# A scan for the routing prefixes, a later weight copy on GpSimd, last tiles one by one, and products that nobody reads on TensorE

## The reference

```python
Y = einsum(where(causal, softmax(Q K^T / 4), 0), V)
x = layernorm(x + Y)
probs = softmax(x @ router^T);  topk_probs, selected = top_k(probs, 2)
topk_probs = topk_probs / max(topk_probs.sum(-1), EPS)
# sort the 8192 choices by expert; keep the 1280 heaviest of each expert
expert_inputs[e, slot] = x[token]
expert_out = ((expert_inputs @ w1^T) * silu(expert_inputs @ wg^T)) @ w2^T
out[token] += expert_out[e, slot] * kept_w
x = layernorm(x + out)
```

## Time and profile before

| | us |
|---|---|
| median of 3 runs | 1727.33 |
| lowest, highest | 1725.76, 1728.22 |
| the profiled execution, its own time | 1726.38 |
| its span in the trace | 1724.6 |
| TensorE busy in the span | 1623.0 (94%) |
| VectorE busy | 1139.5 (66%) |
| ScalarE busy | 1255.3 (73%) |
| GpSimd busy | 300.3 (17%) |

### The profile page before, as it was taken

The page is one execution under the profiler, slowest core; times in us unless marked ns, Lnnn a source line. Parts: engine busy times, 40 slices in busy tenths (PEclk is TensorE's granted clock), DMA queues, the critical chain, the costliest instruction groups (busy, mean ns, idle before and its releaser), DMA issues. The chain is left out here.

```text
span 1724.6 us, 31303 instructions
## 1 busy us (share of the span) xinstructions
PE 1623.0 (94%) x12878; PEld 952.0 (55%) x12878; DVE 1139.5 (66%) x1762; ACT 1255.3 (73%) x1350; POOL 300.3 (17%) x247
## 2 busy tenths in 40 slices
PE   8989999999999999999999994699999999999995
PEld 6823333333333333333333344589998988889884
DVE  7857777777777878777868679345445444644475
ACT  7879999999999999999999986233333333433333
POOL 1000000000000000000310000524243425425144
PEclk9989999999999999999999997899999999999998
DMA  7691030300300303003021003213143323323043
GB/s 252 220 265 56 11 79 1 83 7 1 88 1 3 87 1 78 11 1 88 2 99 50 1 12 111 98 38 107 15 113 68 67 58 68 104 46 92 4 134 121
DMA packets 78385, 118.28 MB, mean 69 GB/s; under 512 B 8690, under 2 KB 62299, under 8 KB 78222
## 3 DMA queue, kind: packets, MB, share of 16 engines
q1 hardware_dynamic: 63328, 98.32, 19.2%
q0 software_dynamic: 14880, 17.82, 5.8%
q10 hardware_dynamic: 32, 0.07, 0.0%
HBM read 80.22 MB, written 40.37 MB: 70 GB/s over the span
## 5 line engine op out<-in xcount | busy, mean ns | idle before, releaser
L975 DVE TENSOR_REDUCE sums<-expq 128x1 f32<-128x1536 f32 (+7 forms) x576 | 559.6, 1034 | 175.7 <-ACT expq L945 175.3
L945 ACT ACTIVATE probs<-scores 128x1536 f32<-128x1536 f32 (+1 forms) x384 | 509.2, 1478 | 8.5 <-PE scores L841 8.4
L945 ACT ACTIVATE expq<-scores 128x1536 f32<-128x1536 f32 x320 | 447.4, 1536 | 2.5 <-PE scores L841 0.9
L863 PE MATMUL o_ps<-probs,v 128*32 128x256 f32 (+1 forms) x4864 | 348.0, 368 | 0.0
L1597 ACT ACTIVATE gate<-up_ps 128x512 f32<-128x512 f32 x128 | 76.6, 598 | 324.8 <-PE up_ps L1434 317.7
L841 PE MATMUL scores<-aq,ak 98*128 98x512 bf16 (+3 forms) x1280 | 304.8, 353 | 7.8 <-PEq L621 6.4
L841 PE MATMUL scores<-ak,aq 98*128 98x512 bf16 (+3 forms) x1184 | 265.1, 343 | 22.7 <-ACT probs L945 16.9
L841 PEld LDWEIGHTS scores<-aq,ak 98*128 98x128 bf16 x1280 | 95.2, 98 | 212.4 <-ACT expq L945 75.5
L1434 PE MATMUL up_ps<-xeT_hi,wup_hi 128*128 128x512 f32 x512 | 203.3, 397 | 3.1 <-DVE xeT_lo L1818 1.4
L1914 DVE TENSOR_TENSOR mid<-up_ps,gate 128x512 f32<-128x512 f32 x128 | 88.4, 691 | 175.8 <-ACT gate L1597 162.0
L1434 PE MATMUL up_ps<-xeT_lo,wup_hi 128*128 128x512 f32 x512 | 202.3, 395 | 0.0
(11 more groups left out here) (269 smaller groups left out, 1903.8 us busy)
## 6 DMA issues: line engine op xcount, KB each, us to landing
raw<-w_T SPq DMA_DIRECT2D x16, 1024.0 KB
split_dram<-parts SPq DMA_DIRECT2D x16, 768.0 KB, 4.8
aq<-split_dram SPq DMA_DIRECT2D x42, 256.0 KB
ak<-split_dram SPq DMA_DIRECT2D x42, 256.0 KB
raw<-wg_T SPq DMA_DIRECT2D x8, 1024.0 KB
v_dram<-vst SPq DMA_DIRECT2D x8, 544.0 KB, 6.8
v<-v_dram SPq DMA_DIRECT2D x8, 544.0 KB, 9.7
xT<-x_T SPq DMA_DIRECT2D x8, 512.0 KB, 6.4
```

The lines of the kernel that those rows point to most:

```text
L863: last = nc.tensor.matmul(o_ps[g % O_RING][32 * h:32 * h + 32, col:col + w], value(gg, k, h, 32), probs[:, m % 2 * GH + h, at:at + w], sta ...
L945: nc.scalar.activation(dst, src[:, 0:w], ACT.Exp, scale=HD ** -0.5).then_inc(exp_done, 1)
L975: last = nc.vector.tensor_reduce(sums[:, gg % 2, col, h:h + 1], expq[:, at % X_RING, lo:lo + w], AX.X, ALU.add)
```

## The change

Five edits, all in the last block:

1. **The places.** `first_prefixes` takes the place of `prefixes` for the first pass. A tensor `by_tile` holds for each expert its base and then the 32 totals; `goes_on` is 1.0 everywhere and 0.0 at the start of each expert. One `tensor_tensor_scan` over 8 x 33 = 264 elements gives in `starts` the base plus the sum of the totals of the earlier tiles. GpSimd fills `goes_on` and the bases at the start of the block (three more instructions, and `iota_ready` is waited for at 11 instead of 8). The sum of all tiles (`total`) is now taken from `starts` in `count_over`.
2. **GpSimd's copy.** `split_down(0, 0)` moves from `keep_ready` to behind the first fetch.
3. **The last tiles** leave as (0, 1), then 2, then 3.
4. **Unread products.** TensorE runs `unread(n)`: n fp32 products of `ident` with the 512 columns of `after` (a constant mask), written to a bank of `up_ps` whose content nobody reads. 3 of them when `logit_off` is there, 14 behind the prefix products, 14 behind the eight list pieces, and 1 behind the first transposes.
5. The branch for an overfull expert, which these inputs don't take, adds the base itself.

```diff
+UNREAD = (3, 14, 14, 1)
...
-        LAST_TILES = ((0, 1), (2, 3))
+        LAST_TILES = ((0, 1), (2,), (3,))
...
+                pool.memset(goes_on[:], 1.0).then_inc(iota_ready, 1)
+                pool.wait_ge(iota_ready, 9)
+                pool.memset(goes_on[:, :, 0:1], 0.0).then_inc(iota_ready, 1)
+                nc.gpsimd.tensor_copy(by_tile[:, :, 0:1], ebase[:][:, :, None]).then_inc(iota_ready, 1)
...
-
-                pool.wait_ge(keep_ready, 1)
-                split_down(0, 0)
...
                 fetch(0, slot_row[:, 0:CT])
+                split_down(0, 0)
                 set_rows(0, 0, 1)
...
+                def unread(n):
+                    for _ in range(n):
+                        nc.tensor.matmul(up_ps[1][:, 1, :], ident[:], after[:].rearrange("p r k -> p (r k)"), start=True, stop=True)
+
+                pe.wait_ge(logit_off, 1)
+                unread(UNREAD[0])
                 pe.wait_ge(keep_ready, 1)
                 prefix_products(ALL).then_inc(prefix_ready, 1)
+                unread(UNREAD[1])
...
+                unread(UNREAD[2])
                 pe.wait_ge(xin_loaded[0], 16 * NA)
                 turn(0, 0)
+                unread(UNREAD[3])
...
+                def first_prefixes(link):
+
+                    dve.wait_ge(prefix_ready, 1)
+                    link(nc.vector.tensor_copy(by_tile[:, :, 1:TT + 1], pf_ps[:, 1, :, :].rearrange("p t e -> p e t")))
+                    link(nc.vector.tensor_tensor_scan(starts[:].rearrange("p e t -> p (e t)"), goes_on[:].rearrange("p e t -> p (e t)"),
+                                                      by_tile[:].rearrange("p e t -> p (e t)"), 0.0, ALU.mult, ALU.add))
+                    link(nc.vector.tensor_tensor(pos[:], starts[:, :, 0:TT].rearrange("p e t -> p t e"), pf_ps[:, 0, :, :], ALU.add))
...
-                    link(nc.vector.tensor_tensor(pos[:, tiles, :], pos[:, tiles, :], each(ebase, tiles), ALU.add))
...
-                    upto_tile = prefixes(link, 1, tiles)
-                    link(nc.vector.tensor_copy(total[:], upto_tile[:, TT - 1, :]))
+                    first_prefixes(link)
                     places(link, tiles)
...
+                    link(nc.vector.tensor_tensor(total[:][:, :, None], starts[:, :, TT:TT + 1], ebase[:][:, :, None], ALU.subtract))
```

More of the change, by code:

```diff
@@ L1130, in program @@
             pos = sb(st, "pos", [P, TT, E])
+            goes_on, by_tile, starts = (sb(st, s, [P, E, TT + 1]) for s in ("goes_on", "by_tile", "starts"))
             total = sb(st, "total", [P, E])
@@ L1696, in route @@
                     nc.vector.tensor_tensor(work[:, of, :], work[:, of, :], wide(red[:, of]), ALU.subtract).then_inc(logit_off, 1)
-                    dve.wait_ge(iota_ready, 8)
+                    dve.wait_ge(iota_ready, 11)
                     dve.wait_ge(logit_off, 1)
@@ L1795, in _ @@
                     weigh(link5, kept_w, kept_w, ALL)
+                    link5(nc.vector.tensor_tensor(pos[:], pos[:], each(ebase, ALL), ALU.add))
                     places(link5, ALL)
```

## The result

| | us |
|---|---|
| before, median of 6 runs | 1726.23 (1724.38 to 1728.22) |
| after, median of 6 runs | 1716.47 (1712.98 to 1719.12) |
| ratio, 95% interval | 0.9944 (0.9934 to 0.9954) |
| after, the profiled execution: its own time, its span | 1717.77, 1716.0 |

The time fell by 9.8 us; the forecast was 1718.0 in a range of 1713.8 to 1721.5. The profiled executions differ by 8.6. Of these, 0.74 lie ahead of the routing's block, which began at 1030.80 us in this execution and at 1031.54 in that of before.

What follows compares the result with a forecast made beforehand. TensorE bounds the experts, the routing's chain across engines the stretch from 1040 to 1110 us. Savings of 3.9 + 0.6 + 2.7 + 1.7 = 8.9 us gave 1717.5 to 1718.4, taken as 1718.0, range 1713.8 to 1721.5.

Steps and rivals of the forecast that it cites:

- 3.9: Routing's lists: VectorE's third `in_q` (marks of the third list piece) moves from 1066.92 to about 1063.0, saving 3.9 us.
- 0.6: First transposes behind the gather: run at the upper clock, they save 0.6 us of a possible 1.0.
- 2.7: First expert's start: fourteen slow up products at 0.232 us each instead of 5.96 us together, saving 2.7 us.
- 1.7: End of the last expert: tiles 2 and 3 leave singly, so the last scatter goes out 1.7 us earlier.
- the forecast had 3.3: TensorE's own gain from the warmer clock, at the transposes and first up products: 3.3 us.
- TensorE's gate: Third `in_q` waits for TensorE's first list piece, held up 2.6 us by unread products and ending at 1063.0.
- VectorE's gate: VectorE's own work, including count and word load, lets the third `in_q` start at 1062.0 to 1062.95.
- 4.16: VectorE's saving up to the first `in_q`, from the moved copy (1.19 us) and the scan (2.97 us).
- The scan: In VectorE's routing chain: 264 elements in 0.7 us; with its copy and sum 1.58 us, saving 2.97 us.
- The clock is held in part: Rival: TensorE's clock falls despite the unread products, in front of prefix products or transposes; 1719.7 to 1721.3 us, chance 0.12.
- The moved copy: GpSimd's copy behind the first fetch costs `xeT_lo` nothing; rival: it holds `xeT_lo` up 1.9 us, 1719.9, chance 0.04.
- The odd pause: 4.6 us between TensorE's last record and VectorE's last tile; rival: it dissolves, 3.7 us more, 1714.3, chance 0.10.

Runs made afterwards that it cites:

- e1: The changed kernel with no unread products at all; median 1722.99 us, ratio 0.9977.
- e6: The kernel before, with only the last expert's last two tiles scattered singly; 1727.28 us, ratio 1.0004.
- e3: The changed kernel with only the unread products behind the lists and the first transposes (14 and 1); median 1721.35 us, ratio 0.9968.
- e5: The kernel before, with only GpSimd's down-weight copy moved behind the first fetch; 1725.93 us against 1727.07, ratio 0.9991.
- e4: The changed kernel with two more unread products behind TensorE's last products; median 1717.73 us, ratio 0.9948.
- e10: The changed kernel, with TensorE waiting for VectorE's reading of the last tile before it leaves the program; 1718.29 us, ratio 0.9956.
- e2: The changed kernel with only the unread products around the prefix products (3 and 14); median 1723.36 us, ratio 0.9981.
- e12: e8 with second-expert up weights held until four gathers land, nine products in the third set, GpSimd pausing after four scatters for TensorE's last signal; 1712.62 us, ratio 0.9919.
- e8: The changed kernel with VectorE's count and flag load moved behind the marks, and ten unread products in the second set; 1715.57 us, ratio 0.9936.
- e11: The changed kernel, with GpSimd's scatters of the last expert's rows begun only behind TensorE's last product's signal; 1718.52 us in one execution.

## Why the prediction was right, and where its terms were off

**The mechanism of the start was right; that the sum was met is in part luck.** The terms were 3.9 + 0.6 + 2.7 + 1.7 = 8.9; in the block they came out at 3.3 + 0.8 + 2.6 + 1.7 = 8.4, by the third `in_q`, the first up product against the third `in_q`, U15 against the first up product, and the way from "taken" to the last scatter. The table has 3.29 for the first; the first up product stood at 71.15 and stands at 67.08; U15 came forward by 6.70.

The medians show two errors of opposite sign. Without unread products (e1) the changed kernel lies 3.8 us under its kernel before, where the forecast's parts for the scan, the copy and the tiles make 5.6. The products bring the rest of the 9.8, about 6, where the forecast had 3.3. Each of these ratios is good to about 1.6 us only, but the two runs' traces name both errors: the 1.7 of the last tiles is eaten by the held signal (e6 gains nothing either), and the branch pauses go with the products.

**The third `in_q`, 3.3 instead of 3.9.** TensorE's gate was forecast well: piece 0 was signalled at 1062.30 plus the 0.74 by which this block began earlier, 1063.04 for 1063.0. VectorE's gate, which I had bounded by 1062.95, was the later one because of the slow load (0.93 for 0.31). VectorE itself saved 3.91 us up to the first `in_q`, not 4.16: the sum of the places takes 0.62 us where I had put 0.42 on it.

**The scan.** 0.71 us for 264 elements; my 0.7 came from twice the time for each element. The Trainium skill ("DVE: opcode table, instruction layouts, handler registers and perf-mode slots", section 6) speaks of half throughput for this scan, and the trace agrees: an operation of 256 elements takes 0.42.

**"The clock is held in part"** happened in its first half: it fell at 1042.5 all the same (PEclk 0.60), and was back at 1046.0, while the three products still ran. It cost nothing, since the prefix products behind them ran at the upper level. e1 to e3 go further: neither set helps the lists at all, as the forecast said of the second (its warmer piece pays only for the products in front of it).

**The moved copy** costs `xeT_lo` nothing, as forecast from the earlier trace rows; the copy of the weights waits 1.77 us with nobody behind it. The rows that show this best are those of e5 and e1, where the low halves run beside the copy for all or nearly all of their length. The Trainium skill ("SBUF — State Buffer", "Who interferes with whom") agrees: these have one SBUF operand, the copy of 10 elements reads and writes SBUF alone.

**The last tiles, 1.7.** Right as a step (1.71), and misleading as a gain: alone (e6) it bought nothing, since the last signal came later by about as much. The two traces with pairs have a hold of 4.49 and 4.55 us; of the ten with one more scatter in front of the last signal, eight have 5.9 to 6.8 (e1, e3, e4 and e6 to e10), the changed kernel's 4.88 and e2's 4.46. **The odd pause** was rightly not expected to dissolve, but I had no cause for it; it is the scatters.

**What the sum left out** and the runs showed: the unread products also move TensorE's code so that no branch waits (1.13 us of pause gone), and beside the second expert's gathers a signal came late (1.10 us of pause new in this trace). From U15 to TensorE's end the two kernels differ by 0.25 us in these traces, so they cancelled. With these 0.25 and a hold that is 0.33 longer, the 8.4 of the terms become the 7.8 by which the block is shorter in the two traces. The median fell by 9.8; the 2.0 left are of the size by which executions of one kernel differ (1713 to 1719), and are not settled.

## What to carry to other kernels

Work for TensorE that nobody reads pays only where the next thing on the path is TensorE's own: behind a fetch it brought 3 us, in front of pieces that another engine gates nothing. A signal that comes long after its last record is a lead worth a run: here holding back GpSimd's indirect transfers around TensorE's last product, and a bulk load that crowded a gather, took another 4 us off the block in the traces (e12 against e8). A gain read from one step of the chain (the 1.7 of the last tiles) has to be tried alone: what gates the next step can move with the edit. And when two kernels that differ in one engine's instruction count differ in a stage that neither edit touches, look at its branches before inventing a mechanism.

## What the runs showed of the hardware

- TensorE's signals can be held beside a row of GpSimd's indirect transfers: the last one by 4.5 to 6.8 us at the end of twelve traces with a scatter every 1.29 us beside it, 0.01 us in the two traces where none (e11) or only four (e12) had gone out before it. The hold sets in behind the third or fourth scatter. Rows of five or six gathers at the same pace in the later experts held none of 209 signals by over 0.26 us.
- A branch of TensorE takes 0.34 us, or 2.0 to 3.8 (13 times, in seven of the fourteen traces); which one is slow goes with the engine's instruction stream. In all seven over 3.3 us a transfer of 16,384 bytes on an instruction queue starts 1.0 us into it.
- A load of one word into VectorE's sequencer took 0.90 to 0.93 us while stores streamed (eight traces), 0.31 without them (six).
- A GpSimd copy held a 10-element SBUF copy of VectorE for up to 2.06 us (e10; 1.77 in the changed kernel), but neither of two operations of 512 columns with one operand in PSUM (e1: 0.69 and 0.70 us beside the copy).
